# Two mixture layers from every expert for every token to tokens grouped by expert

## The reference

```python
x = x + 0.5 * ffn(layernorm(x));  x = x + attn(layernorm(x));  x = x + 0.5 * ffn(layernorm(x))

def ffn(h):                                     # E = 4 experts, D = 256, H = 512
    g = softmax(layer_norm(h, rn_g, rn_b) @ router_w.T)
    top2_w, top2_idx = top_k(g, 2);  top2_w /= sum(top2_w) + 1e-8
    hid = relu(layer_norm(einsum('bsd,edh->bseh', h, w1), ln_g, ln_b))
    expert_out = einsum('bseh,ehd->bsed', hid, w2)
    out = sum(expert_out[top2_idx] * top2_w)
    return layer_norm(out, on_g, on_b)
def attn(x):                                    # 16 heads of 16, no softmax
    Q, K, V = heads(x @ Wq.T + bq), heads(x @ Wk.T + bk), heads(x @ Wv.T + bv)
    return (Q @ cumulative_sum(V outer K)) @ Wo.T + bo
```

## Time and profile before

| | us |
|---|---|
| median of 3 runs | 1239.57 (1239.57 to 1240.85) |
| span of the profiled execution | 1236.4 |
| TensorE busy | 1140.2 |
| VectorE busy | 948.3 |
| GpSimd busy | 672.0 |
| ScalarE busy | 512.8 |

### The profile page before, as it was taken

How to read it: one execution, slowest core, us unless ns; L and a number is a source line. 1 busy time by engine, 2 the same in 40 slices (tenths; PEclk the granted TensorE clock), 3 DMA queues, 4 the chain that set the end, 5 groups by cost and what they waited for, 6 DMA issues and landing times.

```text
span 1236.4 us, 25066 instructions
## 1 busy us (share of the span) xinstructions
PE 1140.2 (92%) x8694; PEld 731.9 (59%) x8694; DVE 948.3 (77%) x2150; ACT 512.8 (41%) x878; POOL 672.0 (54%) x1039
## 2 busy tenths in 40 slices
PE   4669799999999999889999999889999999999996
PEld 4335456656566566656666666556566665666664
DVE  5678787887978878657777777578879787797875
ACT  4353324233342424456665666442333424334131
POOL 2365546454565544498778777543555654546360
PEclk9789989999999999999999999899999999999998
DMA  9002000000000000000000000000000000000000
GB/s 286 4 1 69 1 1 2 1 2 1 0 0 0 1 2 1 19 18 15 11 13 18 17 18 18 1 2 2 17 1 18 1 19 18 0 17 1 19 18 17
DMA packets 29037, 20.69 MB, mean 17 GB/s; under 512 B 7812, under 2 KB 27784, under 8 KB 28808
## 3 DMA queue, kind: packets, MB, share of 16 engines
q1 hardware_dynamic: 24112, 18.36, 5.4%
q10 hardware_dynamic: 4824, 1.07, 0.5%
HBM read 11.03 MB, written 4.19 MB: 12 GB/s over the span
## 4 chain that ended last, share of the span: by engine, by line
PE 48%; DVE 19%; issue 16%; POOL 10%; ACT 4%; DMA 2%; DVEq 1%; ACTq 0%; POOLq 0%
PE bank L1547 7%; PE bank L1549 6%; PE bank L1548 6%; DVE area L674 5%; DVE area L682 4%; PE bank L1532 4%; PE bank L1534 4%; PE bank L1533 4%; DVE area L655 4%; PE bank L1506 4%; POOL area L487 3%; PE bank L1555 2%; PE bank L1557 2%; PE bank L1556 2%; DMA betas<-in_L_ffn_ln_b_dram 2%
## 5 line engine op out<-in xcount | busy, mean ns | idle before, releaser
L1256 ACT ACTIVATE area<-area 128x512 f16<-128x512 f32 x256 | 160.9, 630 | 387.9 <-DVE area L674 386.1
L1547 PE MATMUL bank<-w2h,area 128*128 128x256 f16 x1024 | 281.3, 275 | 12.9 <-DVE area L693 7.2
L1548 PE MATMUL bank<-w2l,area 128*128 128x256 f16 x1024 | 280.5, 274 | 0.0
L1549 PE MATMUL bank<-w2h,area 128*128 128x256 f16 x1024 | 280.5, 274 | 0.0
L674 DVE SCALAR_TENSOR_TENSOR area<-area,betas,bank 128x512 f32<-128x512 f32 x256 | 189.9, 743 | 46.0 <-PE bank L1534 37.6
L682 DVE SCALAR_TENSOR_TENSOR area<-area 128x512 f16<-128x512 f32 x256 | 188.7, 737 | 20.3 <-ACT area L1256 17.1
L1532 PE MATMUL bank<-hTh,w1h 128*128 128x512 f16 x512 | 195.5, 382 | 6.7 <-DVE area L674 6.7
L1533 PE MATMUL bank<-hTl,w1h 128*128 128x512 f16 x512 | 195.1, 381 | 0.0
L1534 PE MATMUL bank<-hTh,w1l 128*128 128x512 f16 x512 | 194.9, 381 | 0.0
L696 DVE SCALAR_TENSOR_TENSOR area<-bank,coef,area 128x256 f32<-128x256 f32 x192 | 92.1, 482 | 79.3 <-PE bank L1549 78.1
L487 POOL TENSOR_TENSOR area<-area 128x512 f16<-128x512 f32 x96 | 119.9, 1274 | 45.1 <-ACT area L1300 44.9
(11 more groups left out here) (233 smaller groups left out, 2109.6 us busy)
## 6 DMA issues: line engine op xcount, KB each, us to landing
X<-in_L_attn_x_dram SPq DMA_DIRECT2D x8, 512.0 KB, 7.1
area<-area SPq DMA_DIRECT2D x128, 32.0 KB, 2.0
out_dram<-X SPq DMA_DIRECT2D x7, 512.0 KB, 2.9
area<-in_L_ffn_w_dram SPq DMA_DIRECT2D x4, 512.0 KB, 9.9
X<-in_L_ffn_w_dram SPq DMA_DIRECT2D x2, 1024.0 KB, 15.7
area<-in_L_ffn_ln_g_dram ACTq DMA_DIRECT2D x1, 1024.0 KB, 6.1
out_dram<-X SPq DMA_DIRECT2D x4, 128.0 KB, 1.7
area<-in_L_attn_Wq_dram SPq DMA_DIRECT2D x1, 256.0 KB, 9.2
```

Source lines behind the costliest of these rows:

```text
L1256: act.activation(Rh[:, e % 2, m, :], V[:, a % NV], ACT.Relu).then_inc(s_Rh, 1)
L1547: pe.matmul(dst, Rh[:, e % 2, k, rows], w2h[:, e, k, :], start=(k == 0), stop=False)
L1548: pe.matmul(dst, Rh[:, e % 2, k, rows], w2l[:, e, k, :], start=False, stop=False)
L1549: last = pe.matmul(dst, Rl[:, e % 2, k, rows], w2h[:, e, k, :], start=False, stop=(k == HC - 1))
```

## The change

The attention's products stay the same; its code is now written out without the loop. What is new is the mixture layer.

*Slots.* A layer is two groups of 16 tiles (2048 tokens). Each token gives two slots, one for each chosen expert. `choose` and the matmuls of `prefix` find, four tiles (a quad) at a time, the place of each slot among its expert's; GpSimd scatters the token's row (high and low part, 1 KB) by indirect DMAs into the expert's region of a DRAM tensor `slots_in`, two DMAs for each tile (`scatter`), and 4 more of zeros behind the regions' ends (`pads`). `tables` gives for each of 35 slot tiles (32, and 3 since each region is rounded up) its row in DRAM (`rtab`) and its expert (`etab`).

*Slot tiles.* SP reads a row number into a register and loads the slot tile. Slot tiles are worked on in pairs, 35 pairs in a layer, written out. TensorE reads two expert numbers (`expert`), and each matmul with expert weights takes its address from that number: base plus number times stride, one register addition, which is why the weights are now 8, 4 and 2 tensors, one for each piece, with the expert as the next dimension. The bias of the hidden layer stands in a row of the product (a row of hT holds the deviation). `layer2`'s output is scaled and stored to `slots_out`.

*Tokens.* For each token tile two indirect DMAs gather its two expert outputs (`gather`, a ring of 2 buffers); ScalarE and VectorE weight and sum them and VectorE finishes the token.

*Order.* Group one is routed before the first pair. In pairs 0 to 12 the second group is routed, in pairs 19 to 28 the first group's tokens are finished, and after pair 34 those of the second. The attention waits for all 32 tiles; its weights, scales and first queries come then.

```diff
-            def layer1(n, par, e, m):
-                a = e * HC + m
-                wait(pe, s_V, NA * n + (a - HC + 1))
-                cols = slice(m * P, (m + 1) * P)
-                o = bank[m][:, :]
-                for c in range(KC):
-                    pe.matmul(o, w1h[:, e, c, cols], hTh[:, par, c, :], start=(c == 0), stop=False)
-                    pe.matmul(o, w1h[:, e, c, cols], hTl[:, par, c, :], start=False, stop=False)
-                    last = pe.matmul(o, w1l[:, e, c, cols], hTh[:, par, c, :], start=False, stop=(c == KC - 1))
+            def expert(S):
+                G, J = group(S)
+                if J == 0:
+                    pe.wait_ge(r_tab, G + 1)
+                return pe.value_load(etab[0:1, G % 2, J:J + 1], min_val=0, max_val=E - 1)
+            def layer1(S, e):
+                p = S // 2
+                pe.wait_ge(b_sdr, p + 1)
+                wait(pe, b_Rl, S - 1)
...
+                a = hT[:, p % R_HT, S % 2]
+                for m in range(HC):
+                    o = bank[S % 2][:, m * P:(m + 1) * P]
+                    for c in range(KC):
+                        pe.matmul(o, w1h[c][m][:, bass.ds(e, 1), :], a[:, c], start=(c == 0), stop=False)
+                        pe.matmul(o, w1h[c][m][:, bass.ds(e, 1), :], a[:, KC + c], start=False, stop=False)
+                        last = pe.matmul(o, w1l[c][m][:, bass.ds(e, 1), :], a[:, c], start=False, stop=(c == KC - 1))
+            def mixture(f):                      # TensorE
...
+                for p in range(NP):
+                    S = 2 * (p0 + p)
+                    if 1 <= p <= GP:
+                        rows_T(u1 + p - 1)
+                    k, odd = divmod(p - 3, 2)
+                    if 0 <= k < GQ and odd:
+                        prefix(Q1 + k)
+                    if p + 1 < NP:
+                        nxt = [expert(S + 2), expert(S + 3)]
+                        grams(p0 + p + 1, nxt)
+                    layer1(S, e[0])
+                    if p + 2 < NP:
+                        slots_T(p0 + p + 2)
+                    if p >= 1:
+                        layer2(S - 1, last)
+                    layer1(S + 1, e[1])
+                    if 1 <= p <= GP:
+                        router(u1 + p - 1)
+                    if p + 1 < NP:
+                        std_T(p0 + p + 1)
+                    layer2(S, e[0])
+                    last, e = e[1], nxt
+            def load_slots(S):                   # SP
...
+                row = sp.value_load(rtab[0:1, G % 2, J:J + 1], min_val=0, max_val=(E - 1) * REG + (GT - 1) * P)
+                sp.dma_start(hs[:, r, k].rearrange("p c d -> p (c d)"),
+                             slots_in[G % 2][bass.ds(row, P), :]).then_inc(l_hs[S % (2 * R_HS)], 16)
+            def gather(i):                       # GpSimd
...
+                wait(pool, c_acc, i - R_C + 1)
+                for k, d in enumerate((yA, yB)):
+                    pool.indirect_dma_start(d[:, i % R_C], None, slots_out[G % 2],
+                                            bass.IndirectOffsetOnAxis(pos[:, G % 2, k, t:t + 1], 0)
+                                            ).then_inc(g_y[i % R_C], 16)
+            def token_sum(i):                    # VectorE
...
+                dve.scalar_tensor_tensor(out=acc[:, r], in0=yB[:, r], scalar=gate[:, G % 2, 1, i % GT:i % GT + 1],
+                                         in1=acc[:, r], op0=ALU.mult, op1=ALU.add).then_inc(c_acc, 1)
+                dve.wait_ge(c_acc, i + 1)
+                step(dve.bn_stats(ast[:, b, :], acc[:, r]))
```

More of the change, by code:

```diff
@@ L359, in _ @@
-            with sp.Fori(NBLK // 2, NBLK - 1, 1) as pair:
-                store(2 * pair)
-            store(2 * NBLK - 2)
-            sp.wait_ge(s_out, 16 * (NBLK - 1 + TB))
+            mixture(1)
+            for i in range(NT):
+                sp.wait_ge(c_x, NT + i + 1)
+                sp.dma_start(out_t[:, i, :], X[:, i, :]).then_inc(s_out, 16)
+            sp.wait_ge(s_out, 16 * NT)
         @block.gpsimd
@@ new lines, in gram_low, with w2_low, chain @@
+                    last.then_inc(p_gl, 1)
+                def w2_low(k):
+                    dve.wait_ge(p_w2h, k + 1)
+                    dve.scalar_tensor_tensor(out=w2l[k][:, :, :], in0=w2r[:, :, k, :], scalar=q2, in1=w2h[k][:, :, :],
+                                             op0=ALU.mult, op1=ALU.subtract).then_inc(p_w2l, 1)
+                def chain(Q):
+                    logits(Q)
+                    choose(Q)
+                    place(Q)
+                rows_low(0)
+                rows_low(1)
@@ L820, in first_block_and_weights @@
+                all_max(1)
+                step(dve.tensor_copy(big[:, 3:4], mxa[:, 1, 0:1]))
+                scales(3, 4)
+                dve.tensor_scalar(kappa, sc[:, 3:4], qi[:, 3:4], None, ALU.mult).then_inc(p_q, 1)
+                chain(1)
+                rows_low(6)
+                rows_low(7)
+                chain(2)
+                for k in range(HC):
+                    w2_low(k)
+                chain(3)
+                tables(0)
                 dve.wait_ge(l_on, 32)
                 dve.tensor_scalar(ong[:, :], ong[:, :], 0.5, None, ALU.mult)
-                at(dve.tensor_scalar(onb[:, :], onb[:, :], 0.5, None, ALU.mult))
@@ L823, in first_block_and_weights, with route @@
-                std_parts(0, at)
-                choose(0, at)
-                weigh(at)
-                coefs(0, 0)
-            def attention_maxima():
+                dve.tensor_scalar(onb[:, :], onb[:, :], 0.5, None, ALU.mult).then_inc(p_on, 1)
+                positions(0)
+                gates(0)
+            def route(G):
+                Q0, u0 = GQ * G, GP * G
+                quad_norm(Q0)
+                for k in range(1, GQ):
+                    quad_norm(Q0 + k)
+                    quad_factors(Q0 + k - 1)
+                quad_factors(Q0 + GQ - 1)
+                for u in range(GP):
+                    rows_low(u0 + u)
+                    if u % 2 == 1 and u >= 3:
+                        logits(Q0 + (u - 3) // 2)
+                        choose(Q0 + (u - 3) // 2)
+                        place(Q0 + (u - 3) // 2)
+                logits(Q0 + GQ - 1)
+                choose(Q0 + GQ - 1)
+                place(Q0 + GQ - 1)
+                tables(G)
@@ L1113, in attention @@
[L1113 to L1134 removed]
+                update_x(NT - 1)
@@ L1137, in _ @@
+            mixture(0)
+            attention()
+            mixture(1)
         @block.scalar
@@ L1478, in weight_T, with rows_out_T @@
+            def rows_out_T(n):
+                wait(pe, s_h, n + 1)
+                wait(pe, a_vf, 2 * n)
+                for c in range(KC):
+                    for t in range(TB):
+                        last = pe.transpose(bank[6 + c][:, t * P:(t + 1) * P], h[:, t, c * P:(c + 1) * P], identf[:, :])
+                    last.then_inc(s_T, 1)
             def weight_T(k):
```

2117 lines of the change are left out of this document (1090 added, 1027 removed).

## The result

The changed kernel takes 1471.05 us (median of 4, 1467.93 to 1475.57) beside 1239.57 (median of 4, 1239.48 to 1240.85) of the kernel before in the same set: 1.1868 times as long, 95% interval 1.1844 to 1.1892. The forecast had 1346, with a range to 1480: the sign was right, and of a loss of 231 us it had foreseen 107. The profiled execution has a span of 1469.4.

The account below looks back on a forecast made before the run. TensorE was taken to bound the mixture layers before the change; heads 127 and 80, pairs 345 twice, tails 62 and 65, prolog 32 and attention 287 gave a span of 1343, 1346 us as a run, range 1205 to 1480.

Parts of the forecast that it names:

- TensorE's saved matmuls: Mixture layers' products: 35 pairs at 6.9 us take 241 us where 8 blocks took 419, 178 less per layer.
- The tails: Last 16 tokens of each layer's second group, after its pairs: 62 us in the first layer, 65 in the second.
- the prolog: Between first mixture layer and attention: preparation that was hidden in the last block, about 32 us.
- the heads: Routing and scatters before each layer's first expert matmul: 127 us in the first layer, about 80 in the second.
- B: Pairs and heads: additions and table loads cost nothing, indirect DMAs 0.7 us; 1219 us as a run; chance 0.22.
- D: Heads and tails: indirect DMAs of 2.5 us make heads 47 longer each, tails 42 each; 1524 us; chance 0.08.
- C: Pairs bound by TensorE's sequencer: addition 0.1, table load 1.3, plain pair 10.9 us; 1524 in all; chance 0.10.
- E: Routing and token pairs: array's work up to twice as long at the slow clock, 54 us; 1400; chance 0.10.
- What a pair costs in fact: Each layer's 35 pairs: routing 10.9, pairs 8 to 11 8.5, plain 8.0, token 12.8 us; 345 a layer.
- The order of `std_parts`: Token pairs: std_parts and std_T, 0.85 us, stand behind the token sums in a chain of 11.3 us, 11.7 with GpSimd's power.
- The sequencer: TensorE in each pair: matmuls 2.3 us, additions 0.06 each, table loads 1.4, 7.3 beside the array's 6.9; plain pair 8.0.
- Attention: The attention keeps its order: 287 of 292 us, as the register loop's edges fall away.

Follow-up runs that it names:

- the best version: Against the changed kernel: slot loads eight slot tiles ahead of the store (before six) and the deviations' rounding ahead of rows and token sums; 1375.03 us.
- set 3: Reruns on one chip: changed kernel 1470.57 us; deviations' rounding moved ahead 1407.83; that plus slot loads ahead 1407.44; slot loads ahead alone 1467.30.

## Why the prediction was right in its sign and half its size

*The structure was right.* TensorE's saved matmuls were real: 246 us a layer at 7.04 a pair, forecast 241. The tails of 62 and 71 us, the prolog of 36 and the heads of 145 and 93 are what was hidden or shorter before, and they came within 0.4, 6, 4 and 13 to 18 us of the forecast. In the first tail two tokens take 7.0 us, as forecast (every second one ends with VectorE's row at 553.20, 560.21 and 567.18); the second tail is long because the end comes 8 us after its last token, not 3. An indirect DMA costs GpSimd 1.27 us from start to start against a forecast of 1.2:

```profile
124.25 0.96 POOL L470 DMA_INDIRECT slots_in<-zrow,padp  x1 [0.30 <-issue]
125.52 0.96 POOL L470 DMA_INDIRECT slots_in<-zrow,padp  x1 [0.31 <-issue]
```

So B, which needed 0.7, was out by this alone, and D, which needed 2.5, as well. C was out too: an addition is 32 ns and mostly hidden, and a table load takes 0.47 us and costs up to 0.9 in a plain pair, not 1.3. (C's 434 us a layer is not worked out from its 10.9 a pair; 35 x 10.9 is 381.) The measured 1471 lies between E at 1400 and C and D at 1524, so that the range holds it only by its upper end, which was drawn for two rivals that fell: that is luck. The Trainium skill's floor of some 600 ns for a tensor_load ("DMA: Bandwidth & Descriptors", "Latency and other measured facts") is above the 0.30 us of the load itself and its 0.47 with what belongs to it, and near the 0.6 that one is worth on average in the best version ((1375.0 - 1292.3) / 140).

*The step that failed* is "What a pair costs in fact": 10.9, 8.5, 8.0 and 12.8 us, where 12.2, 11.3, 9.4 and 14.6 were measured. Five things were mis-sized or missing in it. Their worths are those of single edits; they overlap, and don't add up to the 101 us.

1. The late slot load was missing altogether. I put its two microseconds beside the array's work without asking what stands ahead of it on SP. The load of a pair's second tile stands behind the store of an output that the previous pair makes at its very end. The chain of waits shows it in a token pair, from the scaled output over SP's store and its register work to the load and the transposes:

```profile
363.56 0.48 ACT area L1238
364.05 0.33 SPq L367
364.49 0.27 SPq L358
365.19 2.08 DMA area<-slots_in
367.32 0.40 PE bank L1617 x4
```

Undone, with the deviations first, it is worth 1407.8 - 1375.0 = 33 us; the two kernels ran on two chips, whose controls differ by 2 us.

2. The order of `std_parts` was in the forecast as a chain (11.7 us of a token pair, 9.9 of a routing pair), but a chain priced at full clock, with the half pair behind it on time. Moving two operations of 0.16 us forward was worth 63 us on a chip with the unknown waits, most of it in token pairs, which fell from 14.7 to 11.5 us (routing pairs from 12.3 to 11.4; first layer).

3. The slow clock was rival E, with 54 us and a chance of 0.10, kept out of the sum. It is not a rival but a part of every token pair: keeping the array busy in those 16 gaps gave 1470.6 - 1454.6 = 16 us (two sets on one chip; 27 were expected), and in that kernel the stretch has full clock, and the second layer takes 1.2 us again:

```profile
366.00:470.00 104.00, 85.84 (x921) 71.55 (x920) 60.22 (x183) 31.18 (x57) 49.26 (x52) 1.00 0.26 78
```

```profile
428.66 0.38 PE L1647 MATMUL bank<-ident,s 128*1 128x128 f16 x4 [1.14 <-DVE s L788]
428.98 0.28 PE L1672 MATMUL bank<-w2h,area 128*128 x1
...
430.19 0.27 PE L1674 MATMUL bank<-w2h,area 128*128 x1
```

The rows of before had shown a gap of 6.25 us with the slow clock behind it, and its price; 4 to 5 us of idle time stood in my own sum. With the deviations first the gap is shorter and the granted clock of the token pairs is 0.96 (358.7 to 451.1 in set 3), so part of the 63 us is the clock's. By the Trainium skill ("TensorE: Matmul & The Clock Gate", "HAM oscillation — how this bites in real kernels"), a loop that waits long enough each turn starts each turn cold. The trace agrees: 0.50 behind the wait of 3.9 us in a token pair, and 1.00 over the same pairs with the wait filled.

4. The unknown waits behind TensorE: 21 us by the kernel without the second groups' scatters (1468.6 - 1447.9), and 27 us in the whole between two chips (1467.3 - 1440.1). No row of before could show them.

5. The sequencer, on which the forecast spent most words. It had 1.1 us of a plain pair for 60 additions (3.6) and two loads (1.4), mostly overlapped. Measured is nothing for the additions by themselves, and 1.8 for the two loads with what the additions add behind them, where no other wait covers it. In the changed kernel, where the late slot load does, they are worth 41 / 70 = 0.6 us of a pair. That the mean price of a pair in the best version, 1.2 (82.7 / 70), is near the forecast's 1.1 is luck.

*Heads.* The first scatter came at 76 us where 69 was forecast, since GpSimd's low parts of w1 stand ahead of it; putting them behind gave 1470.6 - 1466.1 = 4.5 us (two sets on one chip), which is not clear of the 3.3 between two equal programs. In both heads there is an unknown wait as well. In the second one VectorE's logits and ScalarE's copy of the rows wait for matmuls that TensorE started by 946.21; this last matmul raises `r_L`, for which both wait, and they go on when a row of scatters has ended:

```profile
946.21 0.17 PE L1545 MATMUL bank<-routw,area 128*128 128x4 f16 x1
...
953.72 0.96 POOL L462 DMA_INDIRECT slots_in<-area,spos  x1 [0.30 <-issue]
957.11 0.23 DVE L666 SCALAR_TENSOR_TENSOR lga<-bank,qi,r 128x16 f32<-128x16 f32 x1 [11.46 <-remote]
957.17 1.02 ACT L1214 ACTIVATE area<-bank 128x1024 f16<-128x1024 f16 x1 [14.09 <-remote]
```

Of the 39 unknown waits of the changed kernel 33 end 1.7 to 2.5 us after the start of the last indirect DMA before.

*Attention.* Its 15 us below the forecast lie at its ends. From VectorE's 13th masked scores to its 109th it takes 209.0 us after and 208.9 before; the stretch ahead of these fell from 29.1 to 23.8 us, and what follows to the last row from 56.9 to 39.6. The last block no longer prepares the next layer, which I had put at 5 us and which stood in a stretch that is 17 shorter now. No run tests this.

What stays open: by which path GpSimd's indirect DMAs hold back TensorE's signals, and why the runs on one of the three chips don't show it.

## What to carry to other kernels

When the bound engine's work is halved, price the loop that is left, not the engine: for each wait in it write down what stands ahead of the releasing instruction in its own queue, stores and tiny operations above all; two operations of 0.16 us in the wrong place cost 63 us here, one store ahead of a load 33. Where such a loop leaves TensorE idle for microseconds, price its matmuls after the gap at the slow clock in the sum itself. Check that an edit changes the distance that it means to change, and keep a control in every set: here an edit that changed nothing looked like a gain of 31 us because it ran in another set, on another chip.

## What the runs showed of the hardware

- Without table loads, register additions between matmuls cost nothing: 1398.2 us without them and 1398.6 with 52 in a pair. A register read from a table takes 0.30 us, 0.47 with its register work. Two of them in a plain pair cost 1.8 us (8.85 and 7.04).
- TensorE's signals reached ScalarE and VectorE late while GpSimd issued indirect DMAs, on two chips of the three on which the sets ran: the waits were 0.8 to 4.6 us long in the pairs, and up to 14.1 in the second head, 11 us after the start of the matmul. Leaving 64 of the 128 scatters out gave back 21 us; in one pair of each layer such waits stand beside gathers alone.
- A kernel with such DMAs took 1.9% and 3.5% longer in one set than in another, on two chips (1440 and 1467 us; 1360 and 1408), where one without them is the same to 0.1% (1239.3 to 1240.0).
